# Differential attention: one maximum over two score banks, and transposes, projection and statistics one unit later

## The reference, cut to what matters

```python
A1 = where(causal, Q1 @ K1.T * scaling, -inf)      # 16 heads, 8 features a map, 256 x 256
A2 = where(causal, Q2 @ K2.T * scaling, -inf)
attn = softmax(A1) - lam * softmax(A2)
O = attn @ V
O = O / sqrt(mean(O * O) + eps) * rms_scale * (1 - LAMBDA_INIT)
x = x + O.reshape(B, N, 256) @ Wo
x = x + ffn(layernorm(x))
x = x + linear_attention(layernorm(x))
x = x + ffn(layernorm(x))
```

## Time and profile before

| | |
|---|---|
| median of 3 runs | 455.25 us (454.56 to 455.97) |
| profiled execution, whole time | 455.39 us |
| its span | 453.3 us |
| PE, DVE, ACT, POOL busy | 386.5, 293.9, 257.0, 203.2 us |
| mean granted TensorE clock | 0.944 of full |
| DVE line 948, 256 maxima on bank 0 | 66.4 us, mean 321 ns, and 36.3 us to read the accumulators |
| DVE line 953, 128 maxima on banks 1 and 2 | 82.9 us, mean 686 ns |

### The profile page before, as it was taken

One profiled execution on the slowest core, in us unless ns is written; L12 is line 12 of the kernel. 1 busy time (PEld: TensorE's weight loads), 2 busy tenths in 40 slices (PEclk: granted clock), 3 DMA queues, 4 the chain that ended last, 5 costly groups with the idle time before them and its releaser, 6 DMA issues.

```text
span 453.3 us, 10148 instructions
## 1 busy us (share of the span) xinstructions
PE 386.5 (85%) x3380; PEld 244.5 (54%) x3380; DVE 293.9 (65%) x1019; ACT 257.0 (57%) x631; POOL 203.2 (45%) x324
## 2 busy tenths in 40 slices
PE   0799689769999888979799798888688999999996
PEld 0566479623455544545455454444475666555674
DVE  6576454169899797989989797110142789999201
ACT  3333134203688777877878686847667433444832
POOL 5223224001558475675848485733001788773000
PEclk9999799955899999999999999956999999999999
DMA  8889969953555434242544400000000000000011
GB/s 205 251 269 309 260 143 235 217 86 46 81 82 82 74 60 76 36 89 35 87 59 75 72 3 3 4 1 0 0 2 1 1 0 2 0 0 2 0 48 46
DMA packets 47347, 34.51 MB, mean 76 GB/s; under 512 B 20032, under 2 KB 41664, under 8 KB 47296
## 3 DMA queue, kind: packets, MB, share of 16 engines
q1 hardware_dynamic: 47296, 33.86, 35.8%
HBM read 25.20 MB, written 8.39 MB: 74 GB/s over the span
## 4 chain that ended last, share of the span: by engine, by line
PE 31%; DVE 26%; issue 9%; ACT 8%; POOL 4%; DMA 1%; DVEq 0%; POOLq 0%; SPq 0%
DVE ps L948 7%; DVE arena L953 7%; PE ps L1258 5%; PE ps L1249 3%; PE ps L1081 3%; PE ps L1461 3%; PE ps L1007 3%; DVE arena L1392 3%; DVE arena L948 2%; PE ps L1157 2%; ACT arena L1202 2%; ACT arena L824 2%; POOL arena L757 2%; PE ps L1002 2%; DVE arena L1405 2%
## 5 line engine op out<-in xcount | busy, mean ns | idle before, releaser
L776 POOL TENSOR_SCALAR_AFFINE_SELECT arena<-arena 128x256 f32<-128x256 f32 (+1 forms) x192 | 90.3, 482 | 97.8 <-ACT arena L824 93.8
L824 ACT ACTIVATE arena<-ps 128x512 f32<-128x512 f32 x192 | 109.5, 604 | 26.0 <-PE ps L1039 25.5
L953 DVE TENSOR_REDUCE arena<-ps 128x2 f32<-128x512 f32 x128 | 82.9, 686 | 6.5 <-PE ps L1015 6.0
L948 DVE CUSTOM_DVE_ANT_0 ps<-ps,future 128x128 f32<-128x128 f32 x256 | 66.4, 321 | 11.9 <-PE ps L1002 11.5
L1039 PE MATMUL ps<-stacks 50*128 50x256 bf16 x256 | 51.4, 281 | 1.2 <-ACT arena L824 1.1
L1333 POOL TENSOR_TENSOR arena<-arena 128x1024 f32<-128x1024 f32 x16 | 34.2, 2134 | 32.6 <-DVE arena L1418 32.1
L1007 PE MATMUL ps<-stacks 48*128 48x256 bf16 x256 | 45.5, 288 | 0.9 <-ACT arena L824 0.5
L391 POOL TENSOR_TENSOR qk_parts_sb<-qk_rest,qk_parts_sb 128x512 bf16<-128x512 f32 x16 | 19.1, 1209 | 51.2 <-DVE qk_parts_sb L491 51.2
L1081 PE MATMUL ps<-arena 128*17 128x256 f32 x512 | 41.4, 396 | 0.0
L1002 PE MATMUL ps<-stacks 48*128 48x128 bf16 x256 | 26.7, 228 | 16.8 <-DVE ps L906 6.1
L948 DVE DVE_READ_ACCUMULATOR2_ANT arena<- 128x1 f32 x256 | 36.3, 142 | 0.0
(11 more groups left out here) (129 smaller groups left out, 750.6 us busy)
## 6 DMA issues: line engine op xcount, KB each, us to landing
stacks<-qk_parts SPq DMA_DIRECT2D x96, 128.0 KB, 4.6
qk_parts<-qk_parts_sb SPq DMA_DIRECT2D x16, 384.0 KB, 4.1
arena<-in_L_ffn_fc_B_dram SPq DMA_DIRECT2D x4, 1024.0 KB, 7.3
arena<-in_L_ffn_fc_A_dram SPq DMA_DIRECT2D x16, 256.0 KB, 4.7
xs<-in_L_attn_a_X_dram SPq DMA_DIRECT2D x4, 256.0 KB, 4.0
qk_parts<-qk_parts_sb SPq DMA_DIRECT2D x8, 128.0 KB, 4.4
stacks<-arena SPq DMA_DIRECT2D x64, 4.0 KB
out_dram<-xs SPq DMA_DIRECT2D x4, 256.0 KB, 2.3
```

The costliest lines, as they stand in the source:

```text
L776: nc.gpsimd.affine_select(out=diag, in_=diag, compare_op=ALU.is_ge, fill=0.0, base=0, pattern=[[0, 2 if s < 2 else UMAPS], [1, P]], channe ...
L824: nc.scalar.activation(probs[:, r, s, :], ps[:, bank, :], ACT.Exp, scale=SCALE).then_inc(exp_done, 1)
L948: last = nc.vector.tensor_tensor_reduce(out=block, in0=block, in1=future[:], scale=1.0, scalar=LOWEST, op0=ALU.add, op1=ALU.max, accum_out ...
L953: last = nc.vector.tensor_reduce(out=rowmax[:, gs, 1, at:at + 2], in_=ps[:, bank, :].rearrange("p (m k) -> p m k", m=2), axis=AX, op=ALU.max)
```

## The change

The two maxima of a unit, over banks 1 and 2, become one instruction over both banks. It waits until both are scored and then signals both as taken (`maxed` goes up by 2 at its end). The sum of squares of slot 3, which stood between the two, comes after it. Three lags go up by one: nT and ACT's copy of it (`L_OPT`, from slot 5 to 6), the projection and the residual (`L_OPROJ`, slot 6 to 7), and the statistics (`L_STAT`, slot 6 to 7). The normalisation itself (`L_NORM`) stays in slot 5. Two numbers are derived from these: `TAIL_OUT` goes from 13 to 14 and the number of drain slots from 15 to 16.

```diff
-L_DEN, L_DIFF, L_SQ, L_MS, L_ROOT, L_NORM, L_OPT, L_OPROJ, L_STAT = 16, 17, 19, 19, 20, 21, 21, 22, 22
+L_DEN, L_DIFF, L_SQ, L_MS, L_ROOT, L_NORM, L_OPT, L_OPROJ, L_STAT = 16, 17, 19, 19, 20, 21, 22, 23, 23
...
-                    for s in range(BANKS_U):
-                        bank = S_BANK + s
-                        dve.wait_ge(scored, BANKS_U * n + s + 1)
-                        if s == 0:
...
-                        else:
-                            at = UMAPS * uu + 2 * s - 2
-                            last = nc.vector.tensor_reduce(
-                                out=rowmax[:, gs, 1, at:at + 2], in_=ps[:, bank, :].rearrange("p (m k) -> p m k", m=2),
-                                axis=AX, op=ALU.max)
-                        last.then_inc(maxed, 1)
-                        if s == 0:
-                            shift_low(it, j)
-                            residual(it, j)
-                        if s == 1:
-                            mean_squares(it, j)
+                    dve.wait_ge(scored, BANKS_U * n + 1)
...
+                    last.then_inc(maxed, 1)
+                    shift_low(it, j)
+                    residual(it, j)
+                    dve.wait_ge(scored, BANKS_U * (n + 1))
+                    nc.vector.tensor_reduce(
+                        out=rowmax[:, gs, 1, UMAPS * uu:UMAPS * (uu + 1)],
+                        in_=ps[:, S_BANK + 1:S_BANK + 3, :].rearrange("p b (m k) -> p (b m) k", m=2),
+                        axis=AX, op=ALU.max).then_inc(maxed, 2)
+                    mean_squares(it, j)
```

More of the change, by code:

```diff
@@ L938, in emit @@
                     uu, gs = j % UPG, j // UPG % 2
-                    for s in range(BANKS_U):
-                        bank = S_BANK + s
-                        dve.wait_ge(scored, BANKS_U * n + s + 1)
-                        if s == 0:
[L944 to L950, removed]
-                        else:
-                            at = UMAPS * uu + 2 * s - 2
-                            last = nc.vector.tensor_reduce(
-                                out=rowmax[:, gs, 1, at:at + 2], in_=ps[:, bank, :].rearrange("p (m k) -> p m k", m=2),
-                                axis=AX, op=ALU.max)
-                        last.then_inc(maxed, 1)
-                        if s == 0:
-                            shift_low(it, j)
-                            residual(it, j)
-                        if s == 1:
-                            mean_squares(it, j)
+                    dve.wait_ge(scored, BANKS_U * n + 1)
+                    carry_wait(dve, tick_dve)
+                    for m in range(UMAPS):
+                        block = ps[:, S_BANK, m * P:(m + 1) * P]
+                        at = UMAPS * uu + m
+                        last = nc.vector.tensor_tensor_reduce(
+                            out=block, in0=block, in1=future[:], scale=1.0, scalar=LOWEST, op0=ALU.add,
+                            op1=ALU.max, accum_out=rowmax[:, gs, 0, at:at + 1])
+                    last.then_inc(maxed, 1)
[7 more added lines that the diff above has]
+                    mean_squares(it, j)
                 else:
```

## The result

The changed kernel took 453.72 us (median of 20 runs, 449.64 to 456.76). The kernel before, run beside it, took 457.0 us (median of 20, 452.41 to 464.26). The ratio is 0.9938, with a 95% interval from 0.9909 to 0.9966: 2.8 us, or 0.6%, faster. The 455.25 us that stood ahead of the prediction was a median of 3 runs and lay at the low side of the 20.

A forecast was written before the change was run, and what follows sets the result against it. DVE (21.17 of 24.30 us a period) and PE (21.11) bound it, in a chain changing between them every slot. 455.39 + 3.2 + 0.4 - 0.1 - 1.0 - 2.3 = 455.6, less 0.14: some 455.4 us; range 451.5 to 458.6.

The forecast's parts named there:

- Part 1: DVE's side: one maximum over two banks takes 1.22 us, not 1.29, saving 0.07 a unit, 4.5 if DVE alone paced.
- Part 2: PE's side: banks come back later; first eight slots cost +3.2 us (0 to 6), full clock +0.4 (-3 to +4).
- "mask sets the pace" term: Full-clock slots: 0.11 us lost in those that a mask set, 0.07 won in those that DVE set.
- Part 3: nT, projection and statistics one slot later: slots 5 to 8 take 11.06 us against 11.08; -0.1 in all (-2.4 to +2.4).
- Part 4: The drain: 1.0 us gained in the last period, 2.3 (0.5 to 5) as rows no longer wait for the projection.
- signs of a wrong forecast: First eight slots keeping 2.3 us, a period under 24.0 or over 24.6, or a drain clock other than before.
- low-clock case: Drain: TensorE's clock stays low and the first feed-forward products start 1.25 us earlier; if it rises, the gain is 4.2.
- The last stretch: Last period: no masked maxima follow the statistics, so 1.0 us is gained (0 to 1.2).
- The forecast: Whole kernel: some 455.4 us for the median, within 0.3% of no change; chance 0.37.
- the rival "faster": Drain and stall give more than first slots cost: 0.2 a period more, 4.2 in the drain, 452.1 us; chance 0.33.
- The slower rival: Loop through both banks sets the pace at full clock too: 0.06 a slot over 56 slots, +3.4, 458.8 us; chance 0.28.
- The 441: Both halves give what they seem to: no stall before nT (7 x 1.42) and 0.07 x 64, 14.4 us less; chance 0.02.

The follow-up runs named there:

- moved steps alone: Kernel before with only the three lags (nT, projection and residual, statistics) raised by one, two single maxima kept: 448.79 us, ratio 0.9848; later 451.36 us, ratio 0.9848.
- statistics alone moved: Kernel before with only the statistics one slot later (L_STAT 23): 454.2 us, ratio 0.9971.
- double from unit 8: Changed kernel, but units 0 to 7 keep two single maxima: 450.27 us, ratio 0.9909 to the kernel before.
- values' copy: Kernel before with the three lags raised, single maxima, and ACT's copy of values in slot 6 instead of 5: 446.16 us, ratio 0.9834 to the kernel before.
- statistics in slot 0: Kernel before with the lags raised, single maxima, and the statistics yet one slot later (L_STAT 24): 450.53 us, ratio 0.9886 to the kernel before.
- factors late: Changed kernel with DVE's feed-forward factors one drain slot later, behind residual and statistics: 456.77 us, ratio 1.0033 to the kernel before.
- double alone: Changed kernel with the lags put back, so only the one maximum over both banks: 462.12 us, ratio 1.0123 to the kernel before.
- factors early: Kernel before with only DVE's feed-forward factors one drain slot earlier: 454.81 us, ratio 1.001.
- values' copy, statistics slot 0: Kernel before with lags raised, single maxima, ACT's copy of values in slot 6 and statistics at L_STAT 24: 449.18 us, ratio 0.9851 to the kernel before.

## Why the prediction was right and wrong

**Part 1 was right.** The double maximum takes 1.223 us; I had estimated 1.22. The estimate from the Trainium skill (Perfetto Trace Analysis, "Optimizing Scalar/DVE Operations") was 0.125 us saved for each instruction taken away. This case shows 1.29 - 1.22 = 0.07, since two maxima one behind the other overlapped already. The section's other advice, to break instructions up where the engine is not saturated and leaves bubbles on others, fits slots 0 to 8: the two single maxima there take back 3.5 us.

**Part 2 had the right loop and too small a size.** A slot takes 2.97 where I had 2.89, and slots 6 and 7 2.97 each where I had 2.85 (a slip: my own loop says 2.89). Slots 0 to 8 cost +4.3 in the profiled pair where I had +3.2; between single profiles it is 3.3 to 4.3. The pair's 4.3 holds 0.5 that is chance: slot 7 to 8 took 3.48 in the kernel before and 3.99 in the changed one, but 3.99 too in the one with the moved steps alone, so the double maximum's own price is 25.28 - 21.45 = 3.8. Nothing of it was caught up. At full clock I took +0.4 in all for the double maximum. It is 0.07 a period with the moved steps, and 0.24 without them, the "mask sets the pace" term: 0.11 in slot 1, as worked out.

**Part 3 was nearly right.** From the masks of slot 5 to the low part of the shift it is 11.03 in the changed kernel (201.22 to 212.25), where my sum said 11.06, and 11.08 before. (By the maxima of slot 5 and the next slot 0 it is 10.87 against 11.12, but the double maximum starts later behind its masks.) The new stall (0.63 to ACT's copy of OT), the copy of values as what delays slot 6, and the wait of 1.09 for the low part of the shift were all as foreseen. The period came out at 24.16 to 24.17, a little under the 24.2 to 24.3 that I had named. The gain of a period is -0.14, where both terms together gave +0.05.

**Part 4 is the step that failed: the drain term was mis-sized.** I took 2.3 between 0.5 and 5. From the last maximum to the squares the profiled pair shows **-4.6**. The rows start at 302.96; I had put them near 302.7, and all my times are 0.39 later in this execution, so the order and its time are right. What was wrong is what follows: I chose the case in which PE's part of the drain stays at the low clock (1.25) over the one in which it rises (4.2), and took a value between them that lies nearer the first. The clock rose at 305.0, as in the kernel before (304.4). The projection then took 1.72 instead of 2.08 and the eight row transposes 1.04 instead of 1.09 and 1.12. The second low stretch of the kernel before (307.8 to 314.6), in which its first products ran, is gone: they took 7.11 instead of 8.95. That the drain's clock would differ was one of my own signs of a wrong forecast. The squares came 4.6 earlier; they did not follow the products, as I had written, but waited 0.79 for POOL (L809), whose work hangs on the last reciprocal (309.73), and that on ACT's last copy of OT. Of the 4.6, 1.4 is lost behind them, where the low clock now falls at 318.6 to 322.0. The place of the factors alone, put back, takes 4.3 to 4.6 us away by the ratios, more than three times the 1.25 of my low-clock case.

The last stretch was predicted at -1.0, with 1.2 as its bound; it is -1.23.

By the terms, then, in this pair: +4.3 for +3.2, -0.8 for +0.3 (some -0.5 of it the late transfers), -1.2 for -1.0, and -4.6 + 1.4 for -2.3. The sum of my terms is +0.2, that of the measured ones -0.9, and the first stage's clock adds -1.8.

The ratios give the drain's size over many executions. The changed kernel is 2.8 faster in spite of 3.8 in slots 0 to 8; 6 x 0.14 and 1.2 are periods and last stretch, so 2.8 + 3.8 - 0.8 - 1.2 = 4.6 is left for the drain. For the moved steps alone it is 7.0 - 6 x 0.21 - 1.2 = 4.5, and undoing the drain's order cost 4.3 to 4.6. Three ways give one number, twice the 2.3 that I took, but they hold the clock.

How much of it is the clock? At the high clock throughout, the stretch from the last maximum to the squares is 29.0 with the moved steps and 30.9 with the statistics alone moved (one profile): 1.9 is order and waits. But single profiles don't size the rest. The low clock between the last maximum and the squares lasts 0 to 20.5 us in those with the moved steps (changed 10 and 0, moved steps 0 and 20.5, double from unit 8 10, values' copy 3, statistics in slot 0 none, both 14, factors late 17) and 0 to 27 in the others (before twice 17, double alone 27, factors early 14, only the statistics moved 0).

The timed runs say more. Each has its mean granted clock on record. The low level is half of the high one, so span x (1 - clock) x 2 is its time at the low level: 33.7 to 78.5 us, differing more between executions of one kernel than between kernels. I fitted all 197 timed runs that have it, with a constant for each kernel and one price for time at the low level. The price is 0.30 us (+-0.02) for each us, and with it the scatter of a run falls from 2.7 to 1.1 us. The estimates, against the kernel before, in us with 95% intervals:

| kernel | mean of all runs | at equal time at the low clock |
|---|---|---|
| changed | -3.4 +-1.1 | -0.9 +-0.5 |
| double alone | +6.0 +-2.3 | +5.1 +-0.9 |
| steps alone | -7.1 +-1.7 | -4.2 +-0.7 |
| double from unit 8 | -6.4 +-1.7 | -3.7 +-0.7 |
| factors early | -2.3 +-1.7 | -0.3 +-0.7 |
| factors late | -0.4 +-1.7 | +1.1 +-0.7 |
| values' copy too | -10.7 +-2.3 | -6.7 +-0.9 |
| statistics alone | -1.7 +-1.7 | +0.2 +-0.7 |
| statistics slot 0 | -6.1 +-2.3 | -2.4 +-0.9 |
| values' copy, statistics slot 0 | -7.7 +-2.3 | -4.9 +-0.9 |

The right column agrees with the traces: 5.1 for the 5.3 of the double maximum alone, 2.5 between steps alone and values' copy for the 2.5 worked out above.

The kernel before spent 55.5 us at the low level (mean of 81 runs), the changed one 47.3 (32 runs): 8.2 less (+-3.1), worth 2.5 us at that price, most of its gain. At equal time at the low clock the drain gives 3.8 - 0.8 - 1.2 + 0.9 = 2.7 in the changed kernel, 4.2 - 1.3 - 1.2 = 1.7 with the moved steps alone, and undoing its order costs 2.0 (+-0.7). So order and waits are worth about the 2.3 that I took; the clock's part, which I had nearly left out by staying close to the low-clock case, is by this estimate some 2 to 3 us more. The fit counts low clock over the whole execution, not in the drain alone, and no run sets the clock by itself. Why the changed kernel has less of it is not shown; the kernels with only the factors early (6.7 less, +-5.0) or only the statistics moved (6.5, +-5.0) have less too.

The forecast: I had seen both halves with opposite signs, and held them for equally large. What came is the rival "faster", nearly by its own reasons: 0.14 a period for its 0.2, and 4.6 in the drain for its 4.2, the clock in it. Its chance stood only 0.04 under the forecast's; working out the drain with PE's queue in both clock cases gave 1.25 and 4.2, and I took a value near the lower without a row that spoke for it. The slower rival's price of 0.06 a slot was too high: it is 0.24 / 8 = 0.03 with the double maximum alone and 0.01 with the steps moved. The 441 did not come: the stall before the transposes turned into the copies', as said against it.

The Trainium skill (TensorE: Matmul & The Clock Gate, "A second HAM failure mode: psum-queue depth-cycling") would, taken to this loop, bring low clock into the periods. The trace disagrees: the granted clock was 1.00 in the period shown, with the stall of 1.09 for the shift in it, as it was before with 1.42.

## What to carry to other kernels

One instruction over two banks gives both back at its end: weigh the fixed cost that it saves (0.07 us here) against the loop with the engine that refills them, first of all where that engine has nothing else to do (0.66 a slot here). A stall hides what is late behind it (here ACT's copy of values, 0.36 a period). In a drain, one instruction in an in-order queue that waits for a shared bank can be worth more than all periods together (2 us against 6 x 0.14 here). Look for these two before the stall itself is priced. Run each half of an edit alone: one half (7 us) was better here than both (2.8). And compare kernels at equal granted clock where each run has it on record: here it explains most of the scatter, and most of the small gain.

## What the runs showed of the hardware

The granted clock in the drain differs between executions of one kernel. In two executions the changed kernel had 10 us of low clock between the last maximum and the squares (31.54 us) and none (28.96). With the moved steps alone it was 20.5 us (35.98) and none (29.06). Over all timed runs each us at the low level goes with 0.30 us (+-0.02) more time. The first maximum, ahead of which the kernels hardly differ (the double one waits some 0.2 for its second mask), came between 92.8 and 97.6 us.

Single transfers of the shift (4 KB each, within the core) come about 1 us late in some periods. In the changed kernel one was issued at 249.29, and PE waits in the same slot where it usually doesn't:

```profile
251.32 0.21 PE L996 MATMUL ps<-stacks 48*128 48x128 bf16 x1 [1.17 <-DVE arena L951]
```

The row names the maximum, which ended at 251.27. But a period earlier the same products started right behind the transposes of OT, beside that maximum and not behind it. Of the 16 parts of the transfer one was complete at 251.24, the others by 249.68. A packet of 16 KB on the instruction queue took 1.1 us near 248.9. That period is 25.13 instead of 24.16. Such packets come about every 10 us throughout, mostly without a late transfer, so this says little; the cause was not tested.
